# Cell products between the chunk sums of a graph network's first pass, on one core

## The reference, cut to what matters

```python
h = relu(layernorm(x))
msg = where(edge_type == 0, h[src] @ W_data.T + b_data, h[src] @ W_control.T + b_control)
x = x + relu(segment_sum(msg, dst) + h @ W_self.T + b_self)
h = relu(layernorm(x))
norm = rsqrt(deg)[src] * rsqrt(deg)[dst]
out = h
for _ in range(2):
    h = segment_sum(h[src] * norm[:, None], dst)
    out = out + h
return x + out / 3
```

## Time and profile before

| what | value |
|---|---|
| device time, median of 3 runs | 4856.43 us (4849.92 to 4858.75) |
| span of the profiled execution | 4840.8 us |
| launch and end around the span, median less span | 15.6 us |
| busy share of the span: PE, PEld, DVE, ACT, POOL | 76%, 62%, 40%, 48%, 59% |
| mean granted TensorE clock | 0.728 |

### The profile page before, as it was taken

One profiled execution on the slowest core, in us unless ns is written; L12 is line 12 of the kernel. 1 busy time (PEld: TensorE's weight loads), 2 busy tenths in 40 slices (PEclk: granted clock), 3 DMA queues, 4 the chain that ended last, 5 costly groups with the idle time before them and its releaser, 6 DMA issues. The chain is left out here.

```text
span 4840.8 us, 59773 instructions
## 1 busy us (share of the span) xinstructions
PE 3663.3 (76%) x22243; PEld 3001.0 (62%) x22243; DVE 1959.6 (40%) x3213; ACT 2307.7 (48%) x3075; POOL 2869.0 (59%) x3055
## 2 busy tenths in 40 slices
PE   7345766677667767666767699898897789998898
PEld 4334444444444444434444688888887688888888
DVE  7213666666666667667666011111112111111111
ACT  4001433333333434334334566666666566666666
POOL 2666665666665666666664556655663565655654
PEclk9555555555555555555556799999998899999999
DMA  5222332323232323233233455555555455555554
GB/s 186 58 53 67 95 92 87 107 90 91 91 107 91 91 91 105 92 95 107 92 103 97 123 149 153 154 156 150 154 151 168 130 148 139 145 144 146 145 144 132
DMA packets 367258, 571.63 MB, mean 118 GB/s; under 512 B 66678, under 2 KB 308225, under 8 KB 359283
## 3 DMA queue, kind: packets, MB, share of 16 engines
q1 hardware_dynamic: 270435, 370.74, 24.4%
q0 software_dynamic: 95664, 196.60, 16.1%
q10 hardware_dynamic: 864, 0.39, 0.0%
HBM read 424.48 MB, written 142.99 MB: 117 GB/s over the span
## 5 line engine op out<-in xcount | busy, mean ns | idle before, releaser
L863 POOL DMA_INDIRECT rows<-typed_table,index x1661 | 1584.4, 954 | 953.6 <-issue 503.1
L863 POOL DMA_INDIRECT rows<-hop_table,index x1306 | 1246.4, 954 | 943.3 <-PE sums_bank L1079 471.2
L999 ACT CAST strip_ring<-stage 128x1792 fp32r<-128x1792 uint8 x840 | 1376.3, 1685 | 751.4 <-remote 384.2
L1188 PE MATMUL wide<-table_parts,strip_ring 128*128 128x256 f32 x11760 | 1567.2, 296 | 112.4 <-issue 60.2
L1188 PEld LDWEIGHTS wide<-table_parts,strip_ring 128*128 128x128 f32 x11760 | 1525.7, 204 | 130.6 <-issue 108.3
L990 ACT CAST stage<-wide 128x392 uint8<-128x392 f32 x1920 | 801.3, 502 | 1356.1 <-PE wide L1150 878.4
L1079 PE MATMUL sums_bank<-hot,rows 128*128 128x80 f32 x5934 | 1095.1, 347 | 291.4 <-issue 240.9
L1150 PE MATMUL wide<-stage 128*128 128x392 bf16 x1920 | 755.1, 490 | 671.6 <-ACT stage L990 309.8
L1079 PEld LDWEIGHTS sums_bank<-hot,rows 128*128 128x128 f32 x5934 | 1047.1, 263 | 328.7 <-issue 325.5
L1150 PEld LDWEIGHTS wide<-stage 128*128 128x128 bf16 x1920 | 185.6, 110 | 1196.7 <-ACT stage L990 525.2
L1550 DVE TENSOR_TENSOR stage<-count_up,stage 128x1568 bf16<-128x1568 f32 x480 | 851.3, 1773 | 0.0
(11 more groups left out here) (140 smaller groups left out, 936.4 us busy)
## 6 DMA issues: line engine op xcount, KB each, us to landing
stage<-strips SPq DMA_DIRECT2D x840, 224.0 KB
strips<-stage SPq DMA_DIRECT2D x60, 1568.0 KB
rows<-typed_table,index POOLq DMA_INDIRECT x1661
rows<-hop_table,index POOLq DMA_INDIRECT x1306
hop_table<-scaled SPq DMA_DIRECT2D x50, 256.0 KB
resid<-xin SPq DMA_DIRECT2D x50, 256.0 KB
xin<-resid SPq DMA_DIRECT2D x50, 256.0 KB
typed_table<-rows SPq DMA_DIRECT2D x49, 256.0 KB, 2.1
```

The costliest lines, as they stand in the source:

```text
L863: pool.indirect_dma_start(out=rows[:, o % RING, c, :], out_offset=None, in_=tables[k], in_offset=bass.IndirectOffsetOnAxis(ap=index[:, chu ...
L999: act.copy(strip_ring[:, number % STRIP_RING], counts_ring[place]).then_inc(strip_cast, 1)
L1188: last = pe.matmul(wide[:, nth % 4, 0:PARTS * P], strip_ring[:, number % STRIP_RING, b - first, :], table_parts[:, b, :, :].rearrange("p n ...
```

## The change

TensorE issues the cells of slot i in slot i+1, spread between the eight chunk sums of that slot's group: after chunk c it issues its share of the 8 or 12 cells. VectorE still makes the quads in slot i, but as the last thing of the slot, behind finish, `take_places` and `take_cells`. ScalarE copies the cells one slot later too: the first four ahead of its part in finish, the others behind it. SyncE stores a strip one slot later.

```diff
+    def quads_used_in(i):
+        return quads_of_slot(i - 1) if i else range(0)
...
-                            for quad in quads_of_slot(i - 1) if i else ():
+                            for quad in quads_used_in(i - 1) if i else ():
                                 if quad % QUADS == QUADS - 1:
                                     store_strip(quad // QUADS)
...
-                        if k == 0 and i < groups:
-                            for quad in quads_of_slot(i):
-                                for w in range(QUAD):
-                                    keep_cell(quad * QUAD + w)
+                        cells = [quad * QUAD + w for quad in (quads_used_in(i) if k == 0 and i < groups else ()) for w in range(QUAD)]
+                        for nth in cells[:QUAD]:
+                            keep_cell(nth)
...
                         if finishing and k == 0:
                             finish(finishing[0], k, finishing[1], True)
+                        for nth in cells[QUAD:]:
+                            keep_cell(nth)
...
-                def sum_group(o):
+                def sum_group(o, cells):
+
                     k, group = places[o]
-                    slot = o % RING
+                    slot, size = o % RING, size_of(group)
                     pe.wait_ge(hot_ready, o + 1)
                     if o >= 2:
                         pe.wait_ge(added, o - 1)
                     pe.wait_ge(rows_landed[slot], landed_by[o])
-                    last = sum_rows(o % 2, slot, size_of(group), hot[:, slot, :, :], WINDOW)
+                    for c in range(size):
+                        last = pe.matmul(sums_bank[:, o % 2, 0:WINDOW], rows[:, slot, c, :], hot[:, slot, c, :],
+                                         start=(c == 0), stop=(c == size - 1))
+                        for nth in cells[c * len(cells) // size:(c + 1) * len(cells) // size]:
+                            make_cell(nth)
                     if k == 0:
-                        last = count_edges(o % 2, size_of(group), hot[:, slot, :, :], WINDOW)
+                        last = count_edges(o % 2, size, hot[:, slot, :, :], WINDOW)
                     last.then_inc(summed, 1)
...
-                def make_cells(quad):
-                    pe.wait_ge(strip_hot_ready, quad + 1)
-                    for w in range(QUAD):
-                        nth = quad * QUAD + w
-                        if nth >= CELL_BANKS:
-                            pe.wait_ge(strip_kept, nth - CELL_BANKS + 1)
+                def make_cell(nth):
+                    quad, w = divmod(nth, QUAD)
+                    if w == 0:
+                        pe.wait_ge(strip_hot_ready, quad + 1)
+                    if nth >= CELL_BANKS:
+                        pe.wait_ge(strip_kept, nth - CELL_BANKS + 1)
...
-                            sum_group(first_of[k] + i)
-                        if k == 0 and i < groups:
-                            for quad in quads_of_slot(i):
-                                make_cells(quad)
-                        elif k and i < hop_groups:
+                            sum_group(first_of[k] + i, [quad * QUAD + w for quad in (quads_used_in(i) if k == 0 else ()) for w in range(QUAD)])
+                        if k and i < hop_groups:
...
                             make_hot(o + 2)
-                        if k == 0 and i < groups:
-                            for quad in quads_of_slot(i):
-                                make_quad(quad)
-                        elif k and 0 < i <= hop_groups:
+                        if k and 0 < i <= hop_groups:
...
                             take_cells(batch_of_slot(cells_turn_slot, i - 1))
+                        if k == 0 and i < groups:
+                            for quad in quads_of_slot(i):
+                                make_quad(quad)
```

More of the change, by code:

```diff
@@ L224, in slot_of_quad @@
         return next(i for i in range(groups) if quads_before(i + 1) > quad)
+    def quads_used_in(i):
+        return quads_of_slot(i - 1) if i else range(0)
+    assert CELL_END + 1 < groups
     typed_table = nc.dram_tensor("typed_table", (2 * real_blocks * P, P), F32, kind="Internal").ap()
@@ L1138, in sum_group @@
                     pe.wait_ge(rows_landed[slot], landed_by[o])
-                    last = sum_rows(o % 2, slot, size_of(group), hot[:, slot, :, :], WINDOW)
+                    for c in range(size):
[3 more added lines that the diff above has]
+                            make_cell(nth)
                     if k == 0:
-                        last = count_edges(o % 2, size_of(group), hot[:, slot, :, :], WINDOW)
+                        last = count_edges(o % 2, size, hot[:, slot, :, :], WINDOW)
                     last.then_inc(summed, 1)
-                def make_cells(quad):
-                    pe.wait_ge(strip_hot_ready, quad + 1)
-                    for w in range(QUAD):
-                        nth = quad * QUAD + w
-                        if nth >= CELL_BANKS:
-                            pe.wait_ge(strip_kept, nth - CELL_BANKS + 1)
-                        pe.matmul(wide[:, nth % CELL_BANKS, 0:real_blocks * CELL], quad_low[quad % 2][:, w, :], quad_hot[quad % 2][:, w, :],
-                                  start=True, stop=True).then_inc(strip_made, 1)
+                def make_cell(nth):
[4 more added lines that the diff above has]
+                        pe.wait_ge(strip_kept, nth - CELL_BANKS + 1)
+                    pe.matmul(wide[:, nth % CELL_BANKS, 0:real_blocks * CELL], quad_low[quad % 2][:, w, :], quad_hot[quad % 2][:, w, :],
+                              start=True, stop=True).then_inc(strip_made, 1)
                 def place_cells(s, reads):
```

## The result

The changed kernel is slower: 5003.57 us median (4986.26 to 5013.73, 4 runs) against 4855.27 us (4849.92 to 4858.75, 4 runs), a ratio of 1.030 with a 95% interval of [1.027, 1.032]. The forecast was 4623 us, and its range ended at 4790.

A forecast was written before the change was run, and what follows sets the result against it. Engines waiting for each other in slots 24 to 205, with GpSimd's pace as ceiling, bound it. A cycle of 74 + 8 + 10.5 = 92.5 us, from 103.7, gave minus 238, plus 5: 4623 us, range 4470 to 4790.

The forecast's parts named there:

- The bound and the place: Slots 24 to 205: engines wait for each other, GpSimd's pace caps any gain at 386 us; hops stay at 2080 us.
- The work: TensorE in slots 24 to 205: 7.9 us a slot, 74 us a cycle of 8.5 slots with turns and places.
- The waits for ScalarE go: TensorE ahead of cells: two chunks, some 2 us, cover a copy's 1.1; idle time falls from 310 to under 100 us.
- Slow stretches: TensorE slow in slots 24 to 205, cause unknown: three quarters stay, 10.5 us a cycle of 8.5 slots.
- The third quad: VectorE's third quad in a slot, made ahead, hides under the second quad's cells: costs nothing; 174 us if uncovered.
- The finish: VectorE's finish, now ahead of its quads: TensorE waits about 8 us a cycle, 6 before, and inside a group.
- rival D: Slower, chance 0.09: fp32 to bf16 switches at each of eight chunk boundaries aren't overlapped; bound 5080 us.
- B: Rival, chance 0.14: the unbroken mix brings TensorE's full clock in the slots, GpSimd alone sets the pace; 4470 us.
- C: Rival, chance 0.14, small gain: the finish delays `summed`, GpSimd stops with its ring full; about 11.9 us a slot, 4800.

## Why the prediction was wrong

**The bound and the place** were right: the hops and the first slots stayed, and the change moved only the middle. **The work** was right in direction. With no gathers the changed slots take 1525 / 182 = 8.4 us; the sum without its slow stretches had (74 + 8) / 8.5 = 9.6. The clock stood at 0.80 there, not at 0.55, and VectorE (7.9 us a slot) was the bound and not TensorE; that the sum came near is in part luck.

**The step that failed is "The waits for ScalarE go".** It priced a cell's way to its copy at 1.1 us, read from undisturbed slots, and gave two chunks, 2 us, as cover. In a slow stretch a cell's cast comes 2.8 to 4.9 us after the one before, so three banks give no cover. The idle time that ScalarE's copies release was to fall below 100 us and rose from 310 to 528. That this wait carries the loss is shown by removal: with it taken out of both, the changed kernel costs no more than the kernel before (both 0.996). What makes the copies late is not the loop: they are late without it too.

**The second failed step is "Slow stretches", kept at three quarters, 10.5 us a cycle.** I sized them as a remainder and took them to be there whatever the order. (The remainder is 12.7 to 13.0 us, not 13 to 14; this slip is worth at most 1 us a cycle.) The price was too small on both sides. Without gathers the kernel before has slots of 1705 / 182 = 9.4 us against 12.2, so gathers cost it some 2.8 x 8.5 = 24 us a cycle; they cost the changed one (2370 - 1525) / 182 x 8.5 = 39, where 10.5 were put. Part of either is GpSimd's own floor of 1836 us. Above that floor stood 386 us, and 534 stand now. The prediction even had the row, and wrote that it didn't know the cause; an unexplained loss was priced as if its cause couldn't meet the change.

How the two meet, as far as the timeline shows: a free slot of 6 us sets two groups free close together, GpSimd gathers both in 20 us without a pause, TensorE falls into 0.70 us steps, and the next slot takes 19. The counts agree. Runs of gathers of over 12 us went from 46 to 67, and of the 71 long slots 36 follow one of under 8 us, where 23 of the 111 others do. The paced runs bear on this link: with pauses for landing there is no such run, and the long slots fall from 71 to 17. That the loop feeds itself in just this way is argued from such counts and not shown by a run of its own.

**The third quad** was priced at nothing. Without gathers that held: VectorE waits 28 us in all ahead of its quads, from 140 before. Beside the gathers it waits 738, from 516, since the cells that it waits for come late. **The finish** was priced at 8 us a cycle. The order alone, in the kernel before, costs 34.5 us, some 1.6 us a cycle over the finish wait of 6 that was there already. The size fits; the wait inside a group, which only the changed kernel has, was not measured by itself.

**The interleaving's switches** (rival D) weren't it. A cell's product takes 443 ns on average, from 490, and a sum's 332, from 397. The side that D stood for came, by another mechanism, and no rival held it. **B** came in part: the clock rose to 0.64, in bursts of 0.96, without paying. In the pair above the clock stood at 0.97 until 1652.8, fell in the gap of 4.16 us, and stood at 0.50 from 1657.3 to 1671.8. The Trainium skill ("TensorE: Matmul & The Clock Gate", Why this matters for your kernels) holds that long idle gaps between bursts cost the full clock, and here the trace agrees. Over the whole stage gaps don't order the two kernels: ahead of cells they sum to 1141 us after the change, against 672, with 88 over 3 us long, against 48, and the granted clock is still the higher one, 0.64 against 0.55. The dense slots between them reach the full level (0.96). **C**'s sign came, GpSimd waiting over 300 us (534), but at 13.0 us a slot and not 11.9.

The rule cited ahead, that matmuls keep program order, held in the pair above: TensorE's next sum product starts at 1657.60, behind the cell of 1657.30, though 4.16 us without a new product lay ahead of that cell.

## What to carry to other kernels

Before moving work between the instructions of another task, price the waits of its ring (here three banks) in the worst stretch of the trace as well as in an undisturbed slot: three banks that are ample at 0.4 us a cell cost 2.8% at 3 us and more. Taking one ring's wait away can hand it to the next, here to VectorE's two buffers. A loss with "issue" ahead of each instruction and no known cause isn't a constant to carry over; find what runs beside it first, which one kernel without the suspected neighbour shows. A step that makes one engine burst can lengthen the bursts of its supplier, so look at the pattern of slots, not only at their mean.

## What the runs showed of the hardware

- **Indirect gathers beside TensorE.** In the slow stretches, which come with long runs of indirect gathers, TensorE finishes one instruction in about 0.70 us, weight load or product. In the pair above the gathers begin at 1644.72; the first late cast, at 1656.75, is that of the cell recorded at 1651.92, so the slowing began between 7 and 12 us in. Over the stage 16 of 1098 copies are late less than 8 us into a run, and 130 of 169 more than 12 us into it. A pause of 2.3 us behind each eight gathers brought the late copies from about 300 to 112; one of 1.2 us left them at 317.
- **Which part of the gather.** Not GpSimd being busy (1552 us with memsets), not the bytes (2358 us with a quarter of each row), not the transfers into the same places (1518 us with plain DMAs), not a long run as such (112 plain DMAs in 60 us). What is left is the indirect form, or the scattered rows that it reads: the plain DMAs read neighbouring ones, and this wasn't separated. The Trainium skill ("DMA: Bandwidth & Descriptors", SWDGE vs HWDGE vs iDMA) says that GpSimd's software writes the descriptors of plain and indirect DMAs alike. By that account the plain run still had software descriptors, and TensorE didn't mind them; the profile agrees as far as both runs have 95664 packets on the queue that it calls software_dynamic. What in the indirect form reaches TensorE stays open.
- **A modelled end.** TensorE's rows put three cells at 1651.92, 1652.28 and 1652.62, while the copies of them came at 1656.75, 1659.58 and 1664.49. The engine that waits for a product dates it better than the product's own row.
